# Four row buffers on each side of the experts instead of two, a fourth norm buffer, and new lags for the order of a two-layer decoder

## The reference

```
t = rmsnorm(x, g2)                         # 2048 tokens
top_v, top_i = top_k(t @ gate_w, 2)        # two of 8 experts for each token
gates = softmax(top_v)
hid = silu(t @ w1[e]); ye = hid @ w2[e]    # w1: 256 x 512, w2: 512 x 256 for each expert
out = sum over the two experts of gates * ye
```

## Time and profile before

| | |
|---|---|
| time, median of 3 runs | 1552.52 us (1545.74 to 1553.4) |
| the profiled execution | 1553.4 us, span 1551.6 us |
| TensorE matmuls busy | 1421.7 us, 92% of the span |
| VectorE busy | 1068.9 us, 69% |
| ScalarE busy | 793.6 us, 51% |
| GpSimd busy | 145.0 us, 9% |
| mean granted clock of TensorE | 0.972 |

### The profile page before, as it was taken

One profiled execution on the slowest core, in us unless ns is written; L12 is line 12 of the kernel. 1 busy time (PEld: TensorE's weight loads), 2 busy tenths in 40 slices (PEclk: granted clock), 3 DMA queues, 4 the chain that ended last, 5 costly groups with the idle time before them and its releaser, 6 DMA issues. The chain is left out here.

```text
span 1551.6 us, 29461 instructions
## 1 busy us (share of the span) xinstructions
PE 1421.7 (92%) x9744; PEld 799.8 (52%) x9744; DVE 1068.9 (69%) x2424; ACT 793.6 (51%) x1512; POOL 145.0 (9%) x166
## 2 busy tenths in 40 slices
PE   6788899999999999999999999999999989898990
PEld 3456576563564445433343343333545545787990
DVE  5786753565564777689999999998768785241415
ACT  5465655536547565555455455555656545332330
POOL 1110120100100001001010000000000021012304
PEclk8899999999999999999999999999999999998995
DMA  7223223501402123133132221111223224965753
GB/s 225 76 72 101 54 74 104 169 8 50 123 32 53 48 79 120 49 91 92 38 99 78 76 83 50 49 47 50 60 53 90 53 84 139 338 225 184 253 183 115
DMA packets 119346, 154.07 MB, mean 99 GB/s; under 512 B 31746, under 2 KB 99714, under 8 KB 117250
## 3 DMA queue, kind: packets, MB, share of 16 engines
q1 hardware_dynamic: 116132, 143.80, 31.1%
q0 software_dynamic: 3072, 8.39, 1.6%
HBM read 73.23 MB, written 18.35 MB: 59 GB/s over the span
## 5 line engine op out<-in xcount | busy, mean ns | idle before, releaser
L1577 ACT ACTIVATE prob<-ps 128x512 f32<-128x512 f32 (+3 forms) x832 | 407.1, 550 | 248.6 <-PE ps L1348 124.1
L1869 DVE TENSOR_REDUCE mx<-ps 128x1 f32<-128x512 f32 (+3 forms) x512 | 281.9, 584 | 89.6 <-PE ps L1315 48.3
L1348 PE MATMUL ps<-of_expert 99*128 99x512 bf16 (+4 forms) x768 | 252.8, 355 | 7.4 <-DMA of_expert<-mrow 6.1
L1348 PEld LDWEIGHTS ps<-of_expert 99*128 99x128 bf16 (+1 forms) x768 | 72.7, 98 | 101.2 <-ACT prob L1577 39.1
L2041 DVE SCALAR_TENSOR_TENSOR room_b<-room_b,ps 128x512 f32<-128x512 f32 x46 | 31.5, 687 | 130.6 <-ACT room_b L1612 113.2
L1385 PE MATMUL ps<-prob,va 128*32 128x512 f32 (+3 forms) x1024 | 115.3, 525 | 0.0
L1313 PE MATMUL ps<-of_expert 102*128 102x512 bf16 x256 | 94.4, 380 | 2.2 <-issue 0.5
L1308 PE MATMUL ps<-of_expert 96*128 96x512 bf16 x256 | 87.6, 384 | 8.1 <-DVE mx L1865 6.9
L1865 DVE CUSTOM_DVE_ANT_0 ps<-ps,room_a 128x512 f32<-128x512 f32 x128 | 86.0, 707 | 4.6 <-PE ps L1308 4.3
L1865 DVE CUSTOM_DVE_ANT_0 ps<-ps,room_b 128x512 f32<-128x512 f32 x128 | 85.8, 708 | 1.1 <-PE ps L1308 0.9
L1305 PE MATMUL ps<-of_expert 96*128 96x128 bf16 (+3 forms) x256 | 71.6, 302 | 9.3 <-DVE mx L1869 7.4
(11 more groups left out here) (219 smaller groups left out, 2620.2 us busy)
## 6 DMA issues: line engine op xcount, KB each, us to landing
of_expert<-parts SPq DMA_DIRECT2D x384, 128.0 KB, 2.4
room_a<-in_w SPq DMA_DIRECT2D x38, 512.0 KB, 5.6
room_b<-in_w SPq DMA_DIRECT2D x18, 512.0 KB, 5.5
otc<-oraw SPq DMA_DIRECT2D x256, 32.0 KB, 2.0
sorted<-y SPq DMA_DIRECT2D x2, 2944.0 KB, 10.4
pack<-sorted SPq DMA_DIRECT2D x46, 128.0 KB
expert_out<-room_b SPq DMA_DIRECT2D x46, 128.0 KB
ct<-in_c SPq DMA_DIRECT2D x8, 512.0 KB, 3.5
```

The lines of the kernel that those rows point to most:

```text
L1348: i = pe.matmul(dst[:, lo:S], ks[0:rows, h, t], qs[0:rows, h, lo:S], start=(a != MASKED), stop=(a != CAUSAL and not fixed))
L1577: act.activation(prob[:, quad % PROBS, n, lo:S], key_bank(*st)[:, lo:S], ACT.Exp).then_inc(s_exp, 1)
L1869: i = dve.tensor_reduce(mx[:, slot, s, n:n + 1], src[:, 0:width], AX.X, ALU.max)
```

## The change

`xin` and `outr` get four buffers each. The two new ones of each lie in `wa`, in the columns of the query weights (`xin`) and the key weights (`outr`). So the load of tile `at` waits for `EH` of tile `at - 4`, and the copy to `outr` for the store of tile `at - 4`; tiles 2 and 3, the first to use the new room, wait instead for the `QK` products of unit 15. Semaphores go from two to four on each side, and a gather waits for all four store semaphores. The norm number 0 gets a buffer of its own (3). The table of lags is replaced as a whole, and with it the order of all steps.

```
+ROWS_IN, ROWS_OUT = 4, 4
 def norm_buffer(n):
-    return {0: 0, 2: 0, 5: 0}.get(n, 1)
+    return {0: 3, 2: 0, 5: 0}.get(n, 1)
...
-            room = [(tile_steps("EH", at - 2), "PE")] if at > 1 else []
+            room = [(tile_steps("EH", at - ROWS_IN), "PE")] if at >= ROWS_IN else [(("QK", UNITS - 1, 0, 0), "PE"), (("QK", UNITS - 1, 0, 1), "PE")] if at > 1 else []
...
-                ("ACT", 0.45, [(tile_steps("ED", at - 2), "SP")] if at > 1 else []), ("SP", 0.6, [], 0.6)]
+                ("ACT", 0.45, [(tile_steps("ED", at - ROWS_OUT), "SP")] if at >= ROWS_OUT else [(("QK", UNITS - 1, 1, 0), "PE"), (("QK", UNITS - 1, 1, 1), "PE")] if at > 1 else []), ("SP", 0.6, [], 0.6)]
...
-LAG = {"IN": -2.9, "EA": -1.2, "CA": 3.7, ("CA", 0): 7.6, ("CA", 1): 16.7, "FS": 7.7, "FZ": 19.8, "SO": 8.5, "OP":
...
-       -0.3, "RZ": -0.9, ("TR", 3): 0.5, "LT": 0.2, ("QK", 3): 3.5, ("SL", 3): 1.1, "OU": 0.2, ("OU", 0): -0.8, "HT":
...
-       "EH": -8.4, ("EH", 0): 8.3, "ED": 0.2, ("EH", 1): 4.9, ("EU", 1): -5.0, ("ED", 1): 17.3}
+LAG = {"IN": -7.5, "CA": 11.2, ("CA", 0): -1.5, ("CA", 1): 17.0, "FS": -0.2, "FZ": 28.1, "SO": -1.1, "OP": -4.8,
...
+       ("EH", 0): 13.4, "EU": 0.4, "ED": -0.9, ("ED", 0): 0.9, ("EH", 1): 3.8, ("EU", 1): 14.6, ("ED", 1): -4.8}
...
-        stats = sb("stats", [P, 3, NT, 6])
+        stats = sb("stats", [P, 4, NT, 6])
...
-        outr = [room_b[:, 3584 + i * D:3584 + (i + 1) * D] for i in range(2)]
-        xin = [pack[:, XIN_AT + i * D:XIN_AT + (i + 1) * D] for i in range(2)]
+        outr = [room_b[:, 3584 + i * D:3584 + (i + 1) * D] for i in range(2)] + [wa[:, (2 + i) * D:(3 + i) * D] for i in range(2)]
+        xin = [pack[:, XIN_AT + i * D:XIN_AT + (i + 1) * D] for i in range(2)] + [wa[:, i * D:(i + 1) * D] for i in range(2)]
...
-                    if at > 1:
-                        sp.wait_ge(s_eh, at - 1)
-                    sp.dma_start(xin[at % 2], xs[k][i * P:(i + 1) * P, :]).then_inc(s_ex[at % 2], 16)
+                    if at >= ROWS_IN:
+                        sp.wait_ge(s_eh, at - ROWS_IN + 1)
+                    elif at > 1:
+                        sp.wait_ge(s_qk, nth("QK", UNITS - 1, 0, 0))
+                        sp.wait_ge(s_qk, nth("QK", UNITS - 1, 0, 1))
+                    sp.dma_start(xin[at % ROWS_IN], xs[k][i * P:(i + 1) * P, :]).then_inc(s_ex[at % ROWS_IN], 16)
...
-                    if at > 1:
-                        act.wait_ge(s_eo[at % 2], 16 * (at // 2))
-                    act.activation(outr[at % 2], side_bank(*st)[:, 0:D], ACT.Copy).then_inc(s_edc, 1)
+                    if at >= ROWS_OUT:
+                        act.wait_ge(s_eo[at % ROWS_OUT], 16 * (at // ROWS_OUT))
+                    elif at > 1:
+                        act.wait_ge(s_qk, nth("QK", UNITS - 1, 1, 0))
+                        act.wait_ge(s_qk, nth("QK", UNITS - 1, 1, 1))
+                    act.activation(outr[at % ROWS_OUT], side_bank(*st)[:, 0:D], ACT.Copy).then_inc(s_edc, 1)
...
-                    for i in range(2):
-                        pool.wait_ge(s_eo[i], 16 * ((sum(TILES[:k + 1]) + 1 - i) // 2))
+                    for i in range(ROWS_OUT):
+                        pool.wait_ge(s_eo[i], 16 * ((sum(TILES[:k + 1]) + ROWS_OUT - 1 - i) // ROWS_OUT))
```

More of the change, by code:

```diff
@@ L547, in parts_of @@
         k = batch_of(b)
-        done = [(("ED", k, TILES[k] - 1), "SP"), (("ED", k, TILES[k] - 2), "SP")]
+        done = [(("ED", k, TILES[k] - 1 - i), "SP") for i in range(ROWS_OUT)]
         i = NT * BATCHES[k].index(b) + t
@@ L785, in decoder @@
         sq = sb("sq", [P, D], BF16)
-        stats = sb("stats", [P, 3, NT, 6])
[L787 to L790, removed]
+        stats = sb("stats", [P, 4, NT, 6])
+        mv = sb("mv", [P, 4, NT, 2])
+        ve = sb("ve", [P, 4, NT])
+        rstd = sb("rstd", [P, 4, NT])
+        shift = sb("shift", [P, 4, NT])
         half = sb("half", [P, NT])
@@ L905, in decoder @@
         s_sx = [sem(f"batch_{k}_sorted") for k in range(len(BATCHES))]
-        s_ex = [sem(f"sorted_tokens_{i}_loaded") for i in range(2)]
-        s_eo = [sem(f"expert_out_{i}_stored") for i in range(2)]
+        s_ex = [sem(f"sorted_tokens_{i}_loaded") for i in range(ROWS_IN)]
+        s_eo = [sem(f"expert_out_{i}_stored") for i in range(ROWS_OUT)]
         s_cg = [sem(f"expert_out_{i}_gathered") for i in range(GATHERS)]
@@ L1140, in _ @@
                     sp.wait_ge(s_edc, at + 1)
-                    sp.dma_start(ys[k][i * P:(i + 1) * P, :], outr[at % 2]).then_inc(s_eo[at % 2], 16)
+                    sp.dma_start(ys[k][i * P:(i + 1) * P, :], outr[at % ROWS_OUT]).then_inc(s_eo[at % ROWS_OUT], 16)
                 elif kind == "SO":
@@ L1420, in _ @@
                     at, dst = tile_at(k, i), side_bank(*st)
-                    pe.wait_ge(s_ex[at % 2], 16 * (at // 2 + 1))
+                    pe.wait_ge(s_ex[at % ROWS_IN], 16 * (at // ROWS_IN + 1))
                     for c in range(NC):
-                        i_ = pe.transpose(dst[:, c * P:(c + 1) * P], xin[at % 2][:, c * P:(c + 1) * P], identf)
+                        i_ = pe.transpose(dst[:, c * P:(c + 1) * P], xin[at % ROWS_IN][:, c * P:(c + 1) * P], identf)
                     i_.then_inc(s_eh, 1)
```

## The result

| | median us (range) | ratio to before, 95% interval | span us |
|---|---|---|---|
| before, timed again beside it | 1548.4 (1545.4 to 1553.4) | | 1551.6 |
| changed | 1543.6 (1540.4 to 1550.1) | **0.9973 [0.9961, 0.9984]** | 1544.7 |

The changed kernel is faster by 0.27%, some 4 us, which is inside the 0.5% that the prediction called no change. The forecast was 1544.5. That the time is met to 1 us is in part luck: the median of before was 1552.5 (3 runs) when the forecast was made and 1548.4 (15 runs, those 3 among them) beside the changed kernel, so of the 8 us forecast as gain some 4 were delivered.

A forecast was written before the change was run, and what follows sets the result against it. TensorE, 92% busy with matmuls, was taken as the bound, so only its idle time, clock or tail could pay. 1553.4 - 3.1 - 1.75 - 2.4 - 0.8 = 1545.3, or 1544.5 against the median 1552.5; range 1533 to 1558.

The forecast's parts named there:

- Output buffers: Turn to batch 1: ScalarE's copy no longer waits for a store, so the hidden product starts earlier, -3.1 us.
- Clock: First hidden product of batch 1: the 4.79 us gap still drops TensorE's clock, so 0 counted; other end -1.8 us.
- Input buffers: First tiles: row load issued two tiles earlier removes a turn's 1.75 us wait for rows, -1.75 us.
- Added waits: Tiles 2 and 3 waiting for unit 15's products, and gather steps waiting for two more semaphores, cost 0.
- norm buffers: Recurrence's norms, first 160 us: a buffer of its own changes who waits for whom, taken as 0.
- The order's chain to batch 1: Last attention heads through router and scatters: a reordered queue starts the chain earlier, shortening the 4.79 us gap, -2.4 us.
- The order in attention: Rest of attention: 77.9 us of small TensorE holes, of which one hundredth is gained, -0.8 us; ends -8 and +8.
- slower rival: Batch 1: additions ahead of the SiLU on VectorE stop TensorE 3.2 us each, five times, giving 1563.7; chance 0.15.
- the whole turn closes: Rival: the gap between batches closes, clock returns and order gains 5 us in attention, giving 1536; chance 0.21.
- Nothing to be measured: Rival: second tile's weights or a slower chain replace the freed copy wait, leaving about 1.75 us, 1551; chance 0.19.
- the signs that the prediction gave: Right if SyncE waits about 12 us or less, the copy waits for no store, product within 1.3 us, tail 35.
- two signs of wrong: A batch 1 product waiting for VectorE's line 2041; attention's last score more than 8 us from where it was.

The follow-up runs named there:

- e7: The kernel before, same step order, lags and norm buffers, with four output buffers and still two input buffers: 1547.1 us, ratio 0.9981 to before.
- e1: The kernel before, same step order, lags and norm buffers, with four input and four output buffers: 1545.0 us, ratio 0.9968 to before.
- e4: The changed kernel with two scatters in flight, each waiting for the one before the last: 1533.9 us, ratio 0.9891 to before.
- e11: Repeat run of the changed kernel with batch 0's additions moved behind the next tile's hidden SiLU of batch 1: 1541.6 us, ratio 0.9946 to before.
- e10: Repeat run of the old step order with four input and four output buffers: 1544.7 us, ratio 0.9960 to before.
- e12: The changed kernel, same order, with the norm buffers of before (numbers 0, 2 and 5 share one): 1547.3 us, ratio 0.9974 to before.
- e9: The changed kernel itself, run again: 1547.4 us, ratio 0.9982 to before.
- e8: The kernel before, unchanged, one execution for a second profile: span 1543.8 us.
- e2: The changed kernel with two input and two output buffers, new lags kept, order the same for the first 2835 of 3199 steps: 1557.5 us, ratio 1.0045 to before.

## Why the prediction was right, and where it was not

*Output buffers, -3.1.* Right: 2.9 us alone (e7), by the mechanism named. ScalarE's copy waits for no store, and from turn to product it is 1.4 us in every kernel with four of them and one scatter at a time. The expected next limit, the second tile's weights, was not it.

*Clock, 0.* Right. The first hidden product still takes 3.73 us in the changed kernel, at a granted clock of 0.50 (window from 1416 to 1419), and 3.28 in e1, after one wait of 8.17 or 6.13 us; with no wait (e4) it takes 2.02, at 1.00. So one gap is enough, which the trace of before could not separate. What is lost is not fixed: over the kernels with one wait of 4.8 to 8.3 us there the product takes 2.98 (e11) to 3.73 us.
The Trainium skill, "TensorE: Matmul & The Clock Gate", section "What's actually happening", says that the throttled clock is the default and recent activity lifts it. By that rule the loss had to stay while the gap stayed and go with it; e4's 2.02 us without a gap agrees.

*Input buffers, -1.75.* Not delivered where it was placed, and as a whole neither shown nor refuted. In the changed kernel no turn of the first tiles waits for rows, but a hidden product there waits 2.57 us for weights, where before had 1.75 us for rows and 0.76 for weights. In the old order four input buffers do not even take the wait for rows away for certain: it is 2.1 us in e10 and absent in e1. The term left out that another load can be what comes last for the same tiles.

*Added waits, 0, and norm buffers, 0.* Nothing speaks against them, by e1 and e12.

*The order's chain to batch 1, -2.4.* This step failed: "each microsecond comes off the 4.79". The chain does start earlier: the first scatter at 1365.1, 1362.3 and 1366.6 (changed, e9, e12) against 1366.0 to 1375.6 with the old order. But what TensorE has behind it is the same 41.2 us, so the end of batch 0 comes earlier by as much. The prediction set the start of the chain against a fixed end of batch 0, though both hang on TensorE's product for the places. Subtracting 1375.55 from 1416.77, and counting the tiles of batch 0 that stand behind `RB` in either order (twelve hidden products in both), would have given it.

*The order in attention, -0.8.* This term was too small. The hastening that the step above has wrongly at the turn belongs here: batch 0 ends at 1405.9 on the average of these three profiles, against 1411.7 of before, e1, e7, e8 and e10, which is -5.8 us, the executions' own differences with it. It is there at the end of attention already: its last score comes at 1302.5 to 1306.7 in the seven profiles with the new order (e2 left out) and at 1306.0 to 1316.0 in the six with the old one, 6.1 us earlier on the average. It is given back behind the turn: from the first hidden product to the last product 93.4, 94.4 and 95.9 us, against 89.1 to 90.7 in the five with the old order, 4.6 us on the average. That is the slower rival's mechanism in the place that the prediction gave it, with its price about right (2.7, 3.8 and 4.3 us a stop, 3.2 forecast; the products that then run slower, 2.73 us instead of 1.89 and 2.90 instead of 1.95, were not in it) and its count wrong: one stop, not five, because once the gathers run they run ahead. It was given 0.15 as a case by itself; it should have been a term of the sum. Its root, the batch's last stores behind SyncE's wait for the scatters, stood in the earlier trace rows, but was read for the copy's sake alone.

Added up: -2.9 for the output buffers, about -2 for the input buffers (by the ratios, without a place in the traces), about 0 for the order as it comes out (-6 and +5, less than the profiles' differences can vouch for to 1 or 2 us; the ratios put the whole change 1 to 3 us behind the old order with four buffers, with intervals that overlap). The forecast had 8; the ratio measured 4. So the total came out by luck: a term of 2.4 that was nothing at the turn, two effects of the new order, -6 and +5 us, that nearly cancel, and a median of before that was 4 us too high. Of the rivals, "the whole turn closes" was right on what a closed turn with a better order is worth (16.5 us forecast, 0.9891 or 16.9 in e4) and wrong that the order could close it: that takes the scatters' own chain, named against it from the earlier trace rows. "Nothing to be measured" has the right sign of its reason (a slower chain in the place of the copy), but the buffers' gain stayed.

Of the signs that the prediction gave, these came as for right: no store is waited for, the product follows the turn by 1.41 us, no turn of the first tiles waits for a load, unit 15's output product is earlier, and the tail is 35.4 us. But SyncE waits 15.9 us in front of batch 1's first load, not 12. And two signs of wrong came with them: a product of batch 1 waits for VectorE (line 2049), and the last score of attention is 13.1 us away from where it was (1302.93 against 1316.04; 1308.07 in e8). The gap at the turn is over 4.8 us, but with scatters that start and end earlier.

Still open: what the input buffers are worth by themselves, and which of the changed lags gives the 6 us in attention.

## What to carry to other kernels

Before a chain that starts earlier is counted as a shorter wait, look for what its start hangs on. If that is a step of the waiting engine itself, the work of that engine behind the step sets the wait: if that work is the same, the wait is too, and only the chain's own steps (here a scatter's wait for the one before) shorten it. When an engine's in-order queue stops for a late DMA, list everything behind it, to the end: a freed buffer upstream only moves the stop on to the next user of what that queue issues. A rival with a clear mechanism and an unsure count belongs in the sum with a count of one.

## What the runs showed of the hardware

- *A chain of eight scatter steps, two indirect DMAs each.* With one step in flight it takes 41.3 to 45.0 us from first to last start, and this spread of 3.7 us alone moves the wait at the turn from 4.8 to 8.3. With two in flight it takes 23.2 to 24.3, with the same weights to load. So it was the landings, waited for in turn, and not bandwidth.
- *Executions of one program differ by more than the effect sought.* Before, twice: span 1551.6 and 1543.8, and the same score product of attention at 1241.9 and 1237.0. The difference grows in steps: 3.5 us at the first output product (141.4 and 137.9), 4.9 at that score product, 7.1 at unit 15's output product (1341.0 and 1333.9) and 7.8 at the end. The profile on which the prediction rests was a long one, 1553.4 where the median beside the changed kernel was 1548.4. What makes the steps isn't known.
